# Layer norms' reciprocal roots computed once per token on GpSimd, between three DMAs, in a two-block Swin kernel

## What is computed

```python
def layer_norm(x, g, b):                       # twice per block, over 64 channels
    mu = jnp.mean(x, axis=-1, keepdims=True); var = jnp.var(x, axis=-1, keepdims=True)
    return (x - mu) * jax.lax.rsqrt(var + EPS) * g + b
...
y = layer_norm(x, ln1_g, ln1_b)                # (rolled by -3, -3 in block 2)
q, k, v = split(windows(y, 7x7) @ qkv_w + qkv_b)      # 8 heads of 8 channels
attn = softmax(q @ k.T * hd**-0.5 + bias (+ mask))
x = x + unwindow(attn @ v) @ proj_w + proj_b
z = layer_norm(x, ln2_g, ln2_b)
x = x + gelu(z @ fc1_w + fc1_b) @ fc2_w + fc2_b
```

## Time and profile before

| | |
|---|---|
| median of three executions | 1196.58 us (1193.92 to 1200.53) |
| span of the profiled execution | 1195.6 us |
| PE, DVE, ACT, POOL busy | 86%, 78%, 42%, 44% of the span |
| attention block 1, MLP block 1, attention block 2, MLP block 2 | about 64 to 480, 480 to 600, 610 to 1023, 1023 to 1130 us |

### The profile page before, as it was taken

One profiled execution on the slowest core, in us unless ns is written; L12 is line 12 of the kernel. 1 busy time (PEld: TensorE's weight loads), 2 busy tenths in 40 slices (PEclk: granted clock), 3 DMA queues, 4 the chain that ended last, 5 costly groups with the idle time before them and its releaser, 6 DMA issues. The chain is left out here.

```text
span 1195.6 us, 24594 instructions
## 1 busy us (share of the span) xinstructions
PE 1034.2 (86%) x8398; PEld 656.2 (55%) x8398; DVE 927.2 (78%) x1427; ACT 500.9 (42%) x1000; POOL 523.4 (44%) x830
## 2 busy tenths in 40 slices
PE   4888887888888878899978888888888879899978
PEld 3554555555555555455545555555555545555548
DVE  3669988888888885888779889887888885888513
ACT  2434444443444433455543445344444433455410
POOL 2134555444445551154464455544445542185500
PEclk9789999988889998899999999988999988999978
DMA  8000000000000000000000000000000000000003
GB/s 187 1 1 1 2 1 0 0 0 0 0 0 0 0 1 1 1 1 0 0 1 2 2 1 0 0 0 0 0 0 0 0 0 2 1 0 0 1 1 108
DMA packets 16833, 9.41 MB, mean 8 GB/s; under 512 B 14228, under 2 KB 16276, under 8 KB 16788
## 3 DMA queue, kind: packets, MB, share of 16 engines
q1 hardware_dynamic: 15776, 6.64, 2.5%
q10 hardware_dynamic: 1012, 2.16, 0.6%
HBM read 5.59 MB, written 3.21 MB: 7 GB/s over the span
## 5 line engine op out<-in xcount | busy, mean ns | idle before, releaser
L350 POOL TENSOR_TENSOR qexp<-qsb,conb 128x392 f32<-128x392 f32 x256 | 234.6, 949 | 52.1 <-ACT qsb L487 50.7
L999 PE MATMUL PS<-qexp,kbd 128*113 128x392 f32 x512 | 240.7, 554 | 6.9 <-issue 5.9
L362 POOL TENSOR_TENSOR osl<-osb,osh 128x392 fp32r<-128x392 f32 x64 | 79.9, 1248 | 368.5 <-ACT osh L525 368.5
L514 ACT ACTIVATE pt<-PS 113x392 f32<-113x392 f32 x256 | 126.8, 496 | 237.7 <-PE PS L999 237.2
L790 DVE TENSOR_SCALAR kexp<-ksb,conb 128x392 fp32r<-128x392 f32 x256 | 205.8, 875 | 9.7 <-ACT ksb L475 9.7
L795 DVE TENSOR_REDUCE nmax<-PS 98x8 f32<-98x392 f32 x256 | 141.0, 561 | 84.1 <-PE PS L999 83.7
L819 DVE RECIPROCAL rec<-PS 128x392 f32<-128x392 f32 x64 | 166.3, 2602 | 27.3 <-PE PS L999 26.4
L999 PE MATMUL PS<-kexp,qbd 128*98 128x392 f32 x256 | 104.9, 410 | 86.2 <-DVE kexp L790 79.2
L999 PE MATMUL PS<-bt,dup_r 113*113 113x392 f32 x256 | 176.3, 689 | 0.0
L999 PE MATMUL PS<-pt,vbd 113*32 113x49 f32 x4096 | 101.3, 219 | 18.4 <-ACT pt L514 9.6
L615 ACT ACTIVATE hid<-PS,vecb 128x392 f32<-128x392 f32 x128 | 75.2, 587 | 100.1 <-PE PS L999 94.7
(11 more groups left out here) (159 smaller groups left out, 1643.0 us busy)
## 6 DMA issues: line engine op xcount, KB each, us to landing
XW<-x_dram SPq DMA_DIRECT2D x14, 196.0 KB, 4.6
out_dram<-XW SPq DMA_DIRECT2D x14, 196.0 KB, 2.4
qexp<-w_dram ACTq DMA_DIRECT2D x2, 384.0 KB, 6.9
conb<-c_all_dram ACTq DMA_DIRECT2D x1, 656.5 KB, 4.4
hid<-c_sel_dram ACTq DMA_DIRECT2D x1, 512.0 KB, 8.1
qexp<-x_dram SPq DMA_DIRECT2D x2, 196.0 KB, 4.5
out_dram<-qexp SPq DMA_DIRECT2D x2, 196.0 KB, 2.4
conb<-c_all_dram ACTq DMA_DIRECT2D x1, 128.0 KB, 2.5
```

What stands on the lines that cost most here:

```text
L350: nc.gpsimd.tensor_tensor(qexp[buf][:, w, :, :], qsb[:, w * NTOK:(w + 1) * NTOK].rearrange("p (a n) -> p a n", a=1).to_broadcast([128, HEA ...
L362: nc.gpsimd.tensor_tensor(osl[:, :], osb[part][:, :], osh[:, :].bitcast(F32), ALU.subtract)\
L514: nc.scalar.activation(pt[w % 4][:, :], bST[w % 2][0:KROWS, 0:HEADS * NTOK], ACT.Exp)\
L999: return nc.tensor.matmul(o, a, b, start=start, stop=stop, **k)
```

## The change

DVE's eight operations are gone from every layer norm; `norm` only waits and multiplies. The reciprocal root is taken once per token and image instead of once per channel:

1. SP waits for `lv[u]` and packs partitions 0 and 64 of it (2 x 392 values) by DMA into `vpk[u]`, 112 partitions of 7 values.
2. POOL raises them to the power -0.5 (`power`, one tensor_tensor of 112x7), into `rpk[u]`.
3. SP writes `rpk[u]` by DMA to `rows[u]` in DRAM.
4. When that has landed, SP spreads the two rows by DMA over 128 partitions into `rstd[u]` (which is `ly` or `lt`), each row read 64 times.
5. DVE waits for it and makes `z[u]`.

SP's part is one program without a loop: 64 times three DMAs, one layer norm after another, each behind the waits of the one before; it stands behind the loads of the start. Core of the diff:

```diff
+            def spread_rstd(h, u, mlp, blk):
+                pair, g = norm_pair(h, mlp, blk), HALVES * blk + 2 * h + u
+                n = 2 * pair + u
+                sp.wait_ge(mvar_used if mlp else var_used, g + 1)
+                sp.dma_start(vpk[u][:, :], lv[u][0::CH, :].rearrange("p (j e) -> p j e", j=PACK // 2)).then_inc(vpk_in[u], 16)
+                sp.wait_ge(pow_done, n + 1)
+                if pair:
+                    sp.wait_ge(rstd_in[u], 16 * pair)
+                sp.dma_start(rows[u].rearrange("w (j e) -> (w j) e", j=PACK // 2), rpk[u][:, :]).then_inc(rows_in, 16)
+                sp.wait_ge(rows_in, 16 * (n + 1))
...
+                sp.dma_start(rstd[u][:, :], bass.AP(rows[u].tensor, 0, [[TOK, 2], [0, CH], [1, TOK]])).then_inc(rstd_in[u], 16)
...
+            def power(h, u, mlp, blk, first=False):
+                pair = norm_pair(h, mlp, blk)
+                pool.wait_ge(vpk_in[u], 16 * (pair + 1))
+                if not first:
+                    pool.wait_ge(rows_in, 16 * (2 * pair + u - 1))
+                nc.gpsimd.tensor_tensor(rpk[u][:, :], vpk[u][:, :],
+                                        wcol[0:PACK, EXPO:EXPO + 1].to_broadcast([PACK, 2 * TOK // PACK]), ALU.pow)\
+                    .then_inc(pow_done, 1)
...
-                ln(nc.vector.tensor_scalar(ly[:, :].bitcast(I32), v[:, :].bitcast(I32), -0.5, MAGIC, ALU.mult, ALU.add))
-                ln(nc.vector.tensor_tensor(lt[:, :], ly[:, :], ly[:, :], ALU.mult))
...
-                nc.vector.tensor_tensor(z[buf][:, :], xps[:, 0:TOK], ly[:, :], ALU.mult).then_inc(done, 1)
+            def norm(h, buf, mlp, blk, xps, done):
+                dve.wait_ge(rstd_in[buf], 16 * (norm_pair(h, mlp, blk) + 1))
+                nc.vector.tensor_tensor(z[buf][:, :], xps[:, 0:TOK], rstd[buf][:, :], ALU.mult).then_inc(done, 1)
...
-                    rowmax(G + 1, 0)
-                    anorm(G + 2, u, {NLINK - 4 + w: (lambda w=w: rowmax(G + 1, w)) for w in range(1, 5)})
-                    for w in range(5, WIN):
-                        rowmax(G + 1, w)
...
+                        rowmax(G + 1, w)
+                        if more2 and w == WIN - 2:
+                            anorm(h + 1, u, blk)
...
                 for u in range(2):
-                    mnorm(base + u + 2, u, {6: lambda: mresidual(u)})
+                    mresidual(u)
+                    mnorm(1, u)
```

More of the change, by code:

```diff
@@ L56 @@
 GROUP = 16
[L57 to L59 removed]
+PACK = 112
 VECTORS = ['ln1_g', 'ln1_b', 'ln2_g', 'ln2_b', 'qkv_b', 'proj_b', 'fc2_b', 'fc1_b']
@@ L152, in build @@
         lt = sb("lt", [128, TOK])
+        rstd = [ly, lt]
+        vpk = [sb(f"vpk{i}", [PACK, 2 * TOK // PACK]) for i in range(2)]
+        rpk = [sb(f"rpk{i}", [PACK, 2 * TOK // PACK]) for i in range(2)]
+        mark = sb("mark", [128, 1])
+        rows = [nc.dram_tensor(f"rows{i}", (2, TOK), F32, kind="Internal").ap() for i in range(2)]
         z = [sb(f"z{i}", [128, TOK]) for i in range(2)]
@@ L379, in attn, with step @@
                     rec[part][:, :].rearrange("p (a n) -> p a n", a=4), ALU.mult).then_inc(att_done, 1)
-            def step(base, g, u, first, more, more2):
+            def step(base, h, u, first, more, more2):
+                g = 2 * h + u
                 if not first:
@@ L411, in _ @@
                 attn(base + HALVES - 1, 1)
+                power(1, 0, 1, blk)
+                power(1, 1, 1, blk)
                 if blk:
                     pool.wait_ge(w_dve, WSTEP["shift"])
-                with pool.Fori(0, PAIRS) as it:
+                with pool.Fori(0, PAIRS - 2) as it:
                     if blk == 0:
@@ L418, in _ @@
                     pool_relay(pool, blk, it)
+                    for u in range(2):
+                        power(it + 2, u, 1, blk)
+                for b in range(PAIRS - 2, PAIRS):
+                    if blk == 0:
+                        pool.wait_ge(mres_done, (b + 1) * 2)
+                    pool_relay(pool, blk, b)
+                    if blk == 0:
+                        power(0, b - PAIRS + 2, 0, 1)
             pool.wait_ge(w_dve, WSTEP["trace"])
@@ L525, in o_copy, with step @@
                 nc.scalar.activation(osh[:, :], bO[part][:, 0:4 * NROWS], ACT.Copy).then_inc(osh_done, 1)
-            def step(p, base, g, u, first, more, more2, tail=None):
+            def step(p, base, h, u, first, more, more2, tail=None):
+                g = 2 * h + u
                 G = base + g
@@ L824, in residual, with step @@
                                                ALU.add, ALU.add).then_inc(res_done, 1)
-            def step(p, blk, base, g, u, first, more, more2, second=False):
+            def step(p, blk, base, h, u, first, more, more2, second=False):
+                g = 2 * h + u
                 G = base + g
@@ L886, in _ @@
                     table(1, 0)
-                step(p, blk, base, 1, 1, False, True, True, second=blk == 0)
+                step(p, blk, base, 0, 1, False, True, True, second=blk == 0)
                 if blk == 0:
```

147 lines of the change are left out of this document (72 added, 75 removed).

## The result

The changed kernel takes 1393.83 us (median of four, 1389.93 to 1395.61) against 1195.25 for the kernel before in the same series (four, 1192.79 to 1200.53): a ratio of 1.164, 95% interval 1.160 to 1.168. Forecast were 1390 us, 1290 to 1465.

The account below looks back on a forecast made before the run. PE was taken to bound the MLP, while in attention it idles for `kexp`. MLP 130, between blocks 8, start 24 and attention 31 sum to 193; 1195.6 + 193 = 1389, by the median 1390 us, range 1290 to 1465.

Parts of the forecast that it names:

- What bounds the kernel: MLP: PE busy throughout; attention: PE idles, its scores waiting 2.98 us for `kexp`, which `recip` and the softmax denominators hold.
- The norm's removal: Attention: taking the norm's operations off DVE gains 0.2 to 0.5 us a step over 28 steps, about 8 us.
- Two engines: Main case, chance 0.85: pack and spread DMAs each run on two of 16 engines; its own range 1305 to 1465 us.
- The first rival: All 16 engines serve pack and spread: spread 2.4 us, MLP step 6.8 us, total 1212 us; chance 0.10.
- the relay: MLP: POOL's relay, one per two steps, was said to fit in beside the chain's loop.
- The links: From `lv` to landed `rstd`: pack 3.1, power 1.4, write 2.0, spread 6.4, handovers 0.2, together 13.1 us.
- The MLP's loop: MLP: pack queues behind the spread, closing a loop of 11.2 us a step against 6.58; +65 us a stage, +130 for both.
- a pack not held up: MLP: if the pack is not held up behind the spread, steps take 9.4 us and the total is 1338 us.
- The start and the stages' beginnings: Start: +24 us, first pack behind bias-table issues; MLP stage beginning: last `osl` queued behind the second power, 6 us late.
- Attention: Attention: eighth row maximum waits for `z`, 2.1 us late, slow steps hide it; about +1.1 a step, +31 us (-8 to +60).
- the four late steps that I allowed for: Attention: four steps after the stages' beginnings, whose `lv` comes later in the step, counted within the +31 us.
- Each 1 us of the power moves the sum by about 50: Whole kernel: each 1 us more or less in POOL's power operation changes the summed loss by about 50 us.

## Why the prediction was right, and where it was not

- **What bounds the kernel.** Right. In the MLP PE was bound by its own work, and by `z` now. The norm's removal was forecast at 0.2 to 0.5 us an attention step; 0.3 was measured with no chain in its place. DVE lost 262 us of work, not 290, which was in no term of the sum.
- **Two engines.** Right, and shown: splitting the spread gave back 159 us, and the DMA row stands at one tenth. The first rival had 1212 us for 16 engines; the nearest to it that was run, with two issues, took 1234.5. Its chain of 8.3 us and not 8.0 makes an MLP step 7.0, and with the stages' late beginnings and the relay the two MLP stages grew by 10.4 and 16.0 us, where the rival had 7 for both.
- **The links.** Mis-sized, against each other: spread 7.4 not 6.4 (94 ns a packet, not 72), its fixed part 1.4 not 1.8; write 1.4 not 2.0; pack 2.0 to 2.5 not 3.1; power 1.48 for 1.4. `lv` to `z` at the start of the second chain is 65.16 less 52.52, 12.6 us, for 13.1. The errors cancelled: that the sum came within 2 us of 193 is in part luck.
- **The MLP's loop.** Right in kind: one pack landing, power, write and spread a step. It measured 0.3 + 1.5 + 1.4 to 1.8 + 7.4 = 10.6 to 11.0, for 11.2 forecast (the write takes 1.8 in every other step; why is open). The relay did not always fit in beside this: once it cost block 2 the 5.9 us above, and that stage grew by 68.0 for 65 although its steps were shorter than forecast. That the pack lines up behind the spread was right, on the engines and from any queue. The sentence that a pack not held up takes 50 us off was not tested: changing its queue did not free it.
- **The start and the stages' beginnings.** +22.1 for +24; `osl` stands behind the power, as said, and PE's wait for it grew from 2.18 to 8.03 us, 5.9 where 6 was the estimate.
- **Attention.** The sum was right (+33.7 for +31), and so was the mechanism, `z` ahead of the eighth row maximum. Its parts were sized wrong. Step by step from `rx` to `rx`, the three later steps that took 25.0 us or less before grew by 1.4 to 1.9 us, near the 2.1 forecast for fast ones, and the eight with a norm that took 26.9 or more grew by 0.3 on average, from -0.9 to +1.1: they hid most of the chain, and gained nothing. All 24 together lost 14, and the first three of each stage 19.6, more than the four late steps that I allowed for.
- **"Each 1 us of the power moves the sum by about 50."** Wrong: 100, for each us 41 in the MLP, where I had 30, and 61 in attention, where I had under 20. The step that failed is that a wait costs attention its own length at most: with the power twice, PE's work went at a lower granted clock as well, 0.84 for 0.94 in the two steps shown. The forecast itself was spared this, since its power was right within 0.1 us.

## What to carry to other kernels

Work that lies beside what bounds a stage costs nothing there, so moving it saves nothing; count what a replacement adds in latency between the producer's end and the consumer's due time, and compare that with the slack (here 8.09 us against 13). Write a broadcast DMA so that its outermost dimension is large, and remember that a small DMA that uses the same few engines can wait behind a large one, here from SP's queue and from ACT's alike. A wait belongs on the in-order engine behind everything that others are waiting for: moving `z` behind `rx` was worth 40 us here.

## What was not expected of the hardware

- A DMA from ACT's queue landed 0.3 us behind the spread from SP's, 6.0 us after its issue, for a 3 KB pack that took 2.0 from SP's queue with no spread under way.
- Splitting a 3 KB DMA into two raised its issue on SP from 0.56 to 1.65 us; splitting the spread of 196 KB raised it from 0.50 to 1.10.
- After a gap of 2.70 us of PE, 3.6 us of its work ran at 0.50 of the full clock in the step shown above. In the changed kernel, behind a gap of 0.93 us at the same place, it ran at 1.00, as its windows view shows (columns as above):

```profile
416.46:420.00 3.54, 3.15 (x54) 2.15 (x56) 3.20 (x3) 1.69 (x4) 1.28 (x2) 1.00 0.00 0
420.00:424.00 4.00, 4.00 (x44) 2.41 (x41) 4.00 (x4) 3.26 (x7) 3.14 (x4) 1.00 0.00 0
```
